# First q and k groups, first x and first masks staged in the q/k stage; V's tile set there by GpSimd

## The chip, the cores and the metric

The kernel runs on one NeuronCore of a Trainium2 chip. Its time is the device time of one execution in microseconds (us), and of several executions the median counts. Engines are named as in the profile: PE is TensorE (PEld its weight loads), DVE is VectorE, ACT is ScalarE, POOL is GpSimd, SP is SyncE, which only issues transfers here. An engine with a q behind its name (SPq, PEq) is its instruction queue.

## The reference, cut to what matters

One layer of a vision tower on an image batch `x` of 4 x 64 x 64 tokens with 64 channels, all in f32:

```
qkv = xw @ qkv_w.T + qkv_b                 # xw: windows of 8x8 tokens, 256 windows, 8 heads of 8
q, k = rope2(q), rope2(k)                  # rotated by row and column inside the window
attn = softmax(q * scale @ k.T)            # 64 x 64 scores per window and head
h = (attn @ v).reshape(...) @ proj_w.T + proj_b
h = h + selective_scan(layernorm(h), W_dbc, W_dt, b_dt, A_log, D)
h = h + one_of_32_experts(layernorm(h))    # routed by argmax
```

The change touches the seam between the first line with the rotation, and the attention.

## The kernel before, in words

The program is a row of blocks (`nc.Block`). Inside a block each engine runs its own instruction list, and they meet by semaphores. At a block's end all five engines meet at a barrier: none starts the next block before the last has finished this one.

**Block 1, the q and k stage (lines 166 to 354).** x is loaded into `h_all` and turned by PE into two SBUF arrays, `xT` (buffer `big_a`) and a column-wise copy in `u_all`. Then PE makes q and k, already rotated, in 32 steps m of two matmuls each (lines 286 and 288). Steps 0 to 15 make the first half of the tokens (q in 0 to 7, k in 8 to 15), steps 16 to 31 the second half. ACT (line 196) and DVE (line 344) each copy one half of the partitions of every step out of PSUM into `qkT` (buffer `big_bc`) and count it in `qk_act` and `qk_dve`. POOL makes the rotated weights `rot` at the block's start (lines 208 to 239) and then has nothing left. SP issues the loads and has nothing left after line 180.

**Block 2, the attention (lines 371 to 724).** It runs over 32 groups of 8 windows, in steps i from -2 to 35, with the groups overlapped: each engine's `body(i)` takes a piece of group i+1, i, i-1 and so on. For a group the order is:

- SP copies q and k of the group from `qkT` into `raw` (`fetch`, line 443: eight transfers, two slots of `raw` by the parity of the group) and x into `x_st` (`fetch_x`, line 453).
- POOL multiplies `raw` by two masks into `k_st` and `q_st` (`masks`, lines 476 and 478). The tiles have one slot, so the masks of group 1 wait for the scores of group 0.
- PE makes the scores (line 518, 16 matmuls, seen as 32 pieces in the profile), DVE takes the maximum (`top`, line 690) and subtracts it (line 695), ACT takes the exponential (line 619), PE turns the result (line 533) and ACT copies that into `prob_t` (line 627).
- PE makes V (line 582) from `x_st`, ACT copies it into `v_st` (line 638), PE multiplies by V (line 549), DVE normalises, PE turns and projects, and the group's h is stored in `h_all`.

`v_st` must hold zeros, with ones in one column per head. DVE sets that at the start of block 2 (lines 680 and 684, counted in `ones_set`), and PE and ACT wait for `ones_set` before anything else there. SP's list in block 2 starts with `fetch(0)`, `fetch(1)`, `fetch_x(0)`; from then on it is `fetch(i+1)`, `fetch_x(i)`. In PE's list the scores of group 0 come first, then V of group 0, then the first turn of group 0, then the scores of group 1.

**Blocks 3 and 4** are the selective scan and the experts. The change does not touch them.

Of the kernel before, what the change touches and what calls it, by code (L numbers as in the profile page):

```python
# [17 lines left out]
F32 = mybir.dt.float32  # L18
I32 = mybir.dt.int32
BF16 = mybir.dt.bfloat16  # L20
ALU = mybir.AluOpType
# [3 lines left out]
P = 128  # L25
# [38 lines left out]
def vit_layer(nc, x, qkv_w, qkv_b, proj_w, proj_b, w_dbc, w_dt, b_dt, a_log, d_skip,  # L64
              router_w, router_b, w1, b1, w2, b2, consts, out):
    ctx = ExitStack()
    with ctx:
# [33 lines left out]

        with ExitStack() as st1:
            def sb1(name, shape, dt=F32):
                return st1.enter_context(nc.sbuf_tensor(name, shape, dt))
# [59 lines left out]
            with nc.Block() as block:  # L166
                @block.sync
                def _(sp):
# [10 lines left out]
                    dup(sp, a_neg, a_log, scan_in)  # L179
                    sp.dma_start(wdt[:, :], w_dt).then_inc(scan_in, 16)  # L180

                @block.scalar
                def _(act):
                    for d in range(2):
                        act.dma_start(wraw[:, d, :], qkv_w[0:2 * C, :]).then_inc(w_in, 16)
                        act.dma_start(wraw2[:, d, :], qkv_w[2 * C:3 * C, :]).then_inc(w_in, 16)
                        act.dma_start(praw[:, d, :], proj_w).then_inc(w_in, 16)
                    act.dma_start(w_ext[C:C + 1, :], proj_b.rearrange("(o d) -> o d", o=1)).then_inc(row_in, 16)
                    act.dma_start(bv_col[:, :], qkv_b[2 * C:3 * C].rearrange("(d o) -> d o", o=1)).then_inc(row_in, 16)
                    act.preload_act_table_set("natural_log_exp_and_others")  # L190
# [12 lines left out]
                @block.gpsimd  # L203
                def _(pool):
# [12 lines left out]
                    for qk in range(2):  # L217
                        for eta in range(2):
                            def part(src):
                                v = src[:, qk * C:qk * C + C].rearrange("p (h e d) -> p h e d", e=2, d=4)  # L220
                                return v[:, :, eta, :].unsqueeze(1).broadcast_to([P, 8, 8, 4])

                            def trig(at):
                                v = kc[:, at:at + 32].rearrange("p (v d) -> p v d", d=4)
                                return v.unsqueeze(2).broadcast_to([P, 8, 8, 4])

                            dst = [rtmp[:, i].rearrange("p v (h d) -> p v h d", d=4) for i in range(2)]
                            pool.tensor_tensor(dst[0], part(w_qkv_t), trig(K_COSR), ALU.mult).then_inc(rot_made, 1)
                            pool.tensor_tensor(dst[1], part(w_swap), trig(K_SINR), ALU.mult).then_inc(rot_made, 1)
                            done += 2  # L230
                            pool.wait_ge(rot_made, done)
                            for w in range(2):
                                q = slice(64 * w, 64 * w + 64)
                                a, b = (rtmp[q, k].rearrange("p v (g n) -> p v g n", g=4) for k in range(2))
                                i = pool.tensor_tensor(rot[q, qk, eta, :, :, w, :], a, b, ALU.add)
                                i.then_inc(rot_made, 1)
                            done += 2
                            pool.wait_ge(rot_made, done)
                            pool.sem_inc(rot_ready, 1)

                @block.tensor
                def _(pe):
# [52 lines left out]
                def _(dve):  # L295
# [54 lines left out]
                    for b in range(2):  # L350
# [5 lines left out]

        attention(nc, dict(kc=kc, h_all=h_all, xT=xT, qkT=qkT, w_v=w_v[:, :].rearrange("p (e n) -> p e n", e=2),
                           w_out=w_out, banks=banks, psum=psum, u_all=u_all))  # L360

# [4 lines left out]
                                  spare=(w_v, w_out), w_delta=w_delta, wd=wd, b_col=b_col, d_col=d_col,  # L366
                                  a_neg=a_neg),
                         (router_w, router_b, w1, b1, w2, b2), out)


def attention(nc, t):
# [4 lines left out]
    with ExitStack() as ctx:  # L376
        def sb(name, shape, dt=F32):
            return ctx.enter_context(nc.sbuf_tensor(name, shape, dt))

        def sem(name):  # L380
            return ctx.enter_context(nc.semaphore(name))

        raw = sb("raw", [P, 2, 2, 4, WIN])
        x_st = sb("x_st", [P, 2, 2, WIN])
        q_st = sb("q_st", [P, 2, 2, P])
        k_st = sb("k_st", [P, 2, 2, 2, WIN])
# [3 lines left out]
        v_st = sb("v_st", [P, 2, 4, 2, 4, 18])  # L390
        inv = sb("inv", [P, 32])
        o_st = sb("o_st", [P, 32, 9])
        o_t = sb("o_t", [72, 4 * P])
# [5 lines left out]
        rstd = sb("rstd", [P, 4])  # L399
        xh = sb("xh", [P, 4, C])  # L400

        power_set, v_zeroed, ones_set = sem("power_set"), sem("v_zeroed"), sem("ones_set")
        qk_staged, x_staged = (sem("qk_staged0"), sem("qk_staged1")), sem("x_staged")
        k_masked, q_masked = sem("k_masked"), sem("q_masked")
# [24 lines left out]
        def first(i, lag=0):  # L429
            return i - lag <= 0  # L430

        with nc.Block() as block:
            @block.sync
            def _(sp):
                def fetch(i, par):

                    if not first(i, 1):
                        sp.wait_ge(k_masked, i - 1)
                        sp.wait_ge(q_masked, i - 1)
                    for eta in range(2):  # L440
                        for g in range(4):
                            a, b = 64 * eta + 16 * g, 32 * g + 16 * eta
                            sp.dma_start(raw[b:b + 16, par, :, :, :].rearrange("p q s k -> p q (s k)"),
                                         qkT[a:a + 16, :, bass.ds(i * 256, 256)]).then_inc(qk_staged[par], 16)

                def fetch_x(i):

                    if not first(i):
                        sp.wait_ge(v_done, i * 2)
                    a = xT[:, bass.ds(i * (2 * WIN) + i // 16 * (L // 2), L // 2 + 2 * WIN)]  # L450
                    src = bass.AP(tensor=a.tensor, offset=a.offset, ap=[list(a.ap[0]), [L // 2, 2], [1, 2 * WIN]],
                                  dep_tracking_offset=a.dep_tracking_offset)
                    sp.dma_start(x_st[:, :, :, :].rearrange("p b f k -> p b (f k)"), src).then_inc(x_staged, 16)

                def body(i, par):
                    if live(i, -1):
                        fetch(i + 1, 1 - par)
                    if live(i, 0):
                        fetch_x(i)

                steps(sp, body)

            @block.gpsimd
            def _(pool):
                pool.memset(mhalf[:, :], -0.5).then_inc(power_set, 1)
                pool.wait_ge(power_set, 1)

                def masks(i, par):

                    pool.wait_ge(qk_staged[par], i // 2 * 128 + 128)  # L470
                    if not first(i):
                        pool.wait_ge(scores_done, i * 4)
                    wide = [P, 4, 2, WIN]
                    head, win = (kc[:, at:at + 2].unsqueeze(1).unsqueeze(3).broadcast_to(wide) for at in (K_HEAD, K_WIN))
                    q, k = (raw[:, par, n].unsqueeze(2).broadcast_to(wide) for n in range(2))
                    pool.tensor_tensor(k_st[:, :, :, :, :].rearrange("p f b h k -> p (f b) h k"), k, head, ALU.mult  # L476
                                       ).then_inc(k_masked, 1)
                    pool.tensor_tensor(q_st[:, :, :, :].rearrange("p f b (w k) -> p (f b) w k", w=2), q, win, ALU.mult  # L478
                                       ).then_inc(q_masked, 1)

                def body(i, par):
                    if live(i, 3):
# [1317 lines left out]
```

## Time and profile before

| | us |
|---|---|
| median of 3 executions | 671.38 (669.72 to 671.96) |
| the profiled execution | 670.87 |
| its span in the profile | 669.1 |
| busy in the span: PE / DVE / ACT / POOL | 571.2 / 503.8 / 419.3 / 307.8 |

The profile lists for one execution when each instruction ran. Beside an instruction it says how long its engine had stood idle before it and what ended that idle time. Busy time of one stage is read from windows of the span. The stages lie roughly so: q and k stage up to 63.9 us, attention up to 337.6 us, then scan, and experts from about 452 us.

### The profile page before, as it was taken

The numbers are of one execution on the slowest core, as the hardware profiler recorded it, in microseconds if no ns is written. First come the engines' busy times: TensorE is split into PE (matmuls) and PEld (weight loads), VectorE is DVE, ScalarE is ACT, GpSimd is POOL, SyncE is SP. The second block draws the span as 40 slices with busy tenths as digits, with TensorE's granted clock in tenths as the row PEclk, the third lists the DMA queues.
The fourth block names the chain that finished last, engine by engine and source line by source line (L and its number), as shares of the span: only waits on it lengthen the run. The fifth ranks groups of instructions, "written<-read, shape, count | busy, mean of one in ns | idle before, by whom it ended". The sixth has DMA issues, their size and how long they took to land. (4 is left out here: it accounts for less than half of the span.)

```text
span 669.1 us, 18246 instructions
## 1 busy us (share of the span) xinstructions
PE 571.2 (85%) x7079; PEld 386.1 (58%) x7080; DVE 503.8 (75%) x879; ACT 419.3 (63%) x723; POOL 307.8 (46%) x352
## 2 busy tenths in 40 slices
PE   3696489999999999999775666757999999999995
PEld 3321378888888888888622122234555555555552
DVE  3798277777777777777379889977777777777772
ACT  3597277777887777787559556713555555555553
POOL 5300235555555555555369659854343332333320
PEclk9798599999999999999977688897999999999999
DMA  9500222222222222221020000000100101001011
GB/s 193 96 1 6 62 56 54 52 50 59 52 55 54 50 52 58 53 51 28 2 28 0 0 1 0 2 2 1 25 21 23 24 20 23 22 22 25 20 23 25
DMA packets 62376, 23.27 MB, mean 35 GB/s; under 512 B 45778, under 2 KB 62162, under 8 KB 62290
## 3 DMA queue, kind: packets, MB, share of 16 engines
q1 hardware_dynamic: 61472, 21.96, 16.2%
q8 instruction: 58, 0.95, 0.6%
q10 hardware_dynamic: 690, 0.13, 0.1%
q14 instruction: 28, 0.23, 0.1%
q0 software_dynamic: 128, 0.00, 0.0%
HBM read 5.29 MB, written 4.19 MB: 14 GB/s over the span
## 5 line engine op out<-in xcount | busy, mean ns | idle before, releaser
L690 DVE TENSOR_REDUCE top<-psum 128x16 f32<-128x1024 f32 x64 | 78.0, 1219 | 61.0 <-PE psum L518 61.0
L627 ACT ACTIVATE prob_t<-psum 128x512 f32<-128x512 f32 x128 | 69.6, 595 | 27.4 <-PE psum L533 27.4
L695 DVE TENSOR_TENSOR prob<-psum,top 128x1024 f32<-128x1024 f32 x64 | 78.4, 1224 | 2.2
L533 PE MATMUL psum<-kc,prob 128*128 128x128 f32 x512 | 69.9, 280 | 11.5 <-ACT prob L619 10.0
L1646 ACT ACTIVATE hid<-psum,b1c 128x512 f32<-128x512 f32 x96 | 59.0, 685 | 32.1 <-PE psum L1553 32.1
L619 ACT ACTIVATE prob<-prob 128x1024 f32<-128x1024 f32 x64 | 67.7, 1058 | 15.8 <-DVE prob L695 15.8
L484 POOL TENSOR_TENSOR rstd<-var,mhalf 128x4 f32<-128x4 f32 x32 | 32.3, 1009 | 85.8 <-DVE var L721 85.8
L1561 PE MATMUL psum<-x_t,w1x 64*64 64x256 f32 x1024 | 70.9, 393 | 0.0
L533 PEld LDWEIGHTS psum<-kc,prob 128*128 128x128 f32 x512 | 55.7, 142 | 21.1 <-ACT prob L619 19.0
L549 PEld LDWEIGHTS psum<-v_st,prob_t 128*64 128x64 f32 x2048 | 62.3, 138 | 6.2 <-ACT prob_t L627 6.1
L1536 POOL TENSOR_TENSOR m_sq<-m_xc 128x256 f32<-128x256 f32 x32 | 19.6, 614 | 99.8 <-DVE m_xc L1697 99.8
L549 PE MATMUL psum<-v_st,prob_t 128*64 128x18 f32 x2048 | 65.5, 212 | 0.0
L1634 PE MATMUL psum<-hid,w2x 128*64 128x256 f32 x512 | 61.4, 382 | 0.4 <-ACT hid L1646 0.4
L518 PE MATMUL psum<-k_st,q_st 32*128 32x128 f32 x1024 | 39.4, 292 | 12.1 <-POOL q_st L478 12.1
L1561 PEld LDWEIGHTS psum<-x_t,w1x 64*64 64x64 f32 x1024 | 33.1, 133 | 19.6 <-issue 11.7
L518 PEld LDWEIGHTS psum<-k_st,q_st 32*128 32x128 f32 x1024 | 33.1, 194 | 17.5 <-issue 17.5
L1538 POOL TENSOR_TENSOR m_rstd<-m_var,m_mhalf 128x4 f32<-128x4 f32 x32 | 32.3, 1008 | 23.6 <-DVE m_var L1711 23.6
L476 POOL TENSOR_TENSOR k_st<-raw,kc 128x512 f32<-128x512 f32 x32 | 33.3, 1042 | 20.5 <-DMA raw<-big_bc 10.3
L638 ACT ACTIVATE v_st<-psum 64x256 f32<-64x256 f32 x64 | 25.4, 398 | 27.3 <-PE psum L582 26.5
L1634 PEld LDWEIGHTS psum<-hid,w2x 128*64 128x64 f32 x512 | 33.8, 136 | 14.6 <-ACT hid L1646 0.6
L1661 ACT ACTIVATE mark_t<-psum 96x512 bf16<-96x512 f32 x32 | 19.0, 593 | 34.5 <-PE psum L1590 34.5
L1718 DVE TENSOR_SCALAR hid<-psum,b1c 128x512 f32<-128x512 f32 x32 | 24.0, 751 | 20.3 <-PE psum L1553 20.3
(200 smaller groups left out, 1280.8 us busy)
## 6 DMA issues: line engine op xcount, KB each, us to landing
raw<-big_bc SPq DMA_DIRECT2D x256, 32.0 KB, 2.0
h_all<-in_x SPq DMA_DIRECT2D x16, 256.0 KB, 5.2
x_st<-big_a SPq DMA_DIRECT2D x32, 128.0 KB, 2.2
out<-out_st SPq DMA_DIRECT2D x128, 32.0 KB
kc<-constants SPq DMA_DIRECT2D x1, 458.0 KB, 4.2
w1x<-in_L_ffn_W SPq DMA_DIRECT2D x2, 128.0 KB, 4.2
w2x<-in_L_ffn_W SPq DMA_DIRECT2D x1, 128.0 KB, 3.8
wraw<-in_L_tok_qkv_w ACTq DMA_DIRECT2D x2, 32.0 KB, 4.6
```

The lines of the kernel that those rows point to most:

```text
L476: pool.tensor_tensor(k_st[:, :, :, :, :].rearrange("p f b h k -> p (f b) h k"), k, head, ALU.mult).then_inc(k_masked, 1)
L484: pool.tensor_tensor(rstd[:, :], var[:, :], mhalf[:, :], ALU.pow).then_inc(rstd_done, 1)
L518: m = pe.matmul(banks[g][:, at:at + P], q_st[q, f, b, :], k_st[q, f, b, :, :], start=True, stop=True, skip_group_check=True)
L533: m = pe.transpose(banks[4 + half][:, n * P:n * P + P], prob[:, f, at:at + 2, :], ident)
L549: m = pe.matmul(banks[6][64 * w:64 * w + 64, at:at + 18], prob_t[:, f, n * 2 + b, 64 * w:64 * w + 64], v_st[:, par, 2 * f + b, w, n, :], s ...
L619: act.activation(prob[:, f], prob[:, f], ACT.Exp).then_inc(prob_done, 1)
L627: act.activation(prob_t[:, f, 4 * half:4 * half + 4, :].rearrange("p j q -> p (j q)"), banks[4 + half][:, :], ACT.Copy).then_inc(prob_t_do ...
L690: dve.tensor_reduce(top[:, f, :].rearrange("p (g h) -> p g h", g=4), sc, AX.X, ALU.max).then_inc(top_done, 1)
L695: dve.tensor_tensor(prob[:, f].rearrange("p (g h) k -> p g h k", g=4), sc, top[:, f, :].rearrange("p (g h) -> p g h", g=4).unsqueeze(3).br ...
L1561: m = pe.matmul(psum[64 * c:64 * c + 64, HID_BANK[g], 256 * b:256 * b + 256], w1x[q, g * 8 + 4 * c:g * 8 + 4 * c + 4, :], x_t[q, i % 2, :, ...
L1634: m = pe.matmul(psum[64 * b:64 * b + 64, 6, 0:256], w2x[:, g, :], hid[:, g, 256 * b:256 * b + 256], start=False, stop=(g == 3), skip_group ...
L1646: act.activation(hid[:, g, :], psum[:, HID_BANK[g], :], ACT.Relu, bias=b1c[:, g:g + 1]).then_inc(relu_act, 1)
```

## The change

Tiles and semaphores that both blocks now use are made outside block 1: `raw`, `x_st`, `q_st`, `k_st`, `v_st` (`sb0`, freed after the attention), and `qk_staged`, `x_staged`, `k_masked`, `q_masked`, `v_zeroed`, `ones_set`. The bodies of `fetch`, `fetch_x` and `masks` become functions `fetch_qk`, `fetch_x` and `mask_qk` without their waits. In block 1, SP waits until steps 0 to 15 of q and k are stored, and then issues both first groups' q and k and the first x. POOL sets `v_st` behind `rot`, waits for the first group's eight transfers and masks it. In block 2 these steps are left out.

```diff
@@ block 1, SP
+                    sp.wait_ge(qk_act, 16)
+                    sp.wait_ge(qk_dve, 16)
+                    for i in range(2):
+                        fetch_qk(sp, at, i)
+                    fetch_x(sp, at, 0)
@@ block 1, POOL, behind rot
+                    v_st = at["v_st"]
+                    pool.memset(v_st[:, :, :, :, :, :], 0.0).then_inc(at["v_zeroed"], 1)
+                    pool.wait_ge(at["v_zeroed"], 1)
+                    for e in range(2):
+                        ones = v_st[64 * e:64 * e + 64, :, :, :, :, 9 * e + 8:9 * e + 9]
+                        pool.memset(ones.rearrange("p a s w n o -> p (a s w n) o"), 1.0).then_inc(at["ones_set"], 1)
+                    pool.wait_ge(at["ones_set"], 2)
+                    pool.wait_ge(at["qk_staged"][0], 128)
+                    mask_qk(pool, at, 0)
@@ block 2, SP
-                def body(i, par):
-                    if live(i, -1):
-                        fetch(i + 1, 1 - par)
-                    if live(i, 0):
-                        fetch_x(i)
+                def body(i, par):
+                    if live(i, -1) and i >= 1:
+                        sp.wait_ge(k_masked, i)
+                        sp.wait_ge(q_masked, i)
+                        fetch_qk(sp, t, i + 1)
+                    if live(i, 0) and i >= 1:
                         sp.wait_ge(v_done, i * 2)
+                        fetch_x(sp, t, i)
@@ block 2, POOL
-                    if live(i, -2):
-                        masks(i + 2, par)
+                    if live(i, -2) and i >= -1:
+                        pool.wait_ge(qk_staged[par], (i + 2) // 2 * 128 + 128)
+                        pool.wait_ge(scores_done, i * 4 + 8)
+                        mask_qk(pool, t, i + 2)
@@ block 2, DVE
-                dve.memset(v_st[:, :, :, :, :, :], 0.0).then_inc(v_zeroed, 1)
-                dve.wait_ge(v_zeroed, 1)
-                for e in range(2):
-                    ones = v_st[64 * e:64 * e + 64, :, :, :, :, 9 * e + 8:9 * e + 9]
-                    dve.memset(ones.rearrange("p a s w n o -> p (a s w n) o"), 1.0).then_inc(ones_set, 1)
```

SP's list around the barrier between block 1 and block 2 (the two branches), before:

```order
L180 DMA wdt<-in_L0_attn_W_dt 16x64
L166 UNCONDITIONAL_BRANCH
L433 UNCONDITIONAL_BRANCH
L443 DMA raw<-big_bc 16x2x256 x16
L453 DMA x_st<-big_a 128x2x128
L443 DMA raw<-big_bc 16x2x256 x8
```

and now:

```order
L191 DMA wdt<-in_L0_attn_W_dt 16x64
L405 DMA raw<-big_bc 16x2x256 x16
L414 DMA x_st<-big_a 128x2x128
L177 UNCONDITIONAL_BRANCH
L486 UNCONDITIONAL_BRANCH
L405 DMA raw<-big_bc 16x2x256 x8
```

The 16 transfers of q and k and the one of x stand ahead of the branches now, and block 2 starts with the eight of group 2.

POOL's list at the same place, from the last piece of `rot` on, before:

```order
L235 TENSOR_TENSOR rot<-rtmp 64x32x8 x2
L166 UNCONDITIONAL_BRANCH
L463 UNCONDITIONAL_BRANCH
L465 MEMSET mhalf 128x4
L476 TENSOR_TENSOR k_st<-raw,kc 128x512
L478 TENSOR_TENSOR q_st<-raw,kc 128x512
```

and now:

```order
L252 TENSOR_TENSOR rot<-rtmp 64x32x8 x2
L259 MEMSET v_st 128x1152
L263 MEMSET v_st 64x64 x2
L423 TENSOR_TENSOR k_st<-raw,kc 128x512
L425 TENSOR_TENSOR q_st<-raw,kc 128x512
L177 UNCONDITIONAL_BRANCH
L499 UNCONDITIONAL_BRANCH
L501 MEMSET mhalf 128x4
L423 TENSOR_TENSOR k_st<-raw,kc 128x512
```

The three memsets of `v_st` and the masks of group 0 moved ahead of the branches; behind `mhalf` the masks of group 1 come first. The lists of PE and ACT keep their order, and DVE's loses the memsets alone.

## Rows read from the trace of the kernel before

**Rows 1.** Windows by stage: us, then each engine's busy time, PE's granted clock.

```profile
core 0: us, PE busy (x) PEld busy (x) DVE busy (x) ACT busy (x) POOL busy (x), PEclk, DMA share, GB/s
47.00:63.00 16.00, 13.42 (x58) 3.83 (x54) 15.48 (x19) 15.34 (x18) 0.00 (x0) 1.00 0.00 1
63.00:72.00 9.00, 0.00 (x0) 0.00 (x0) 1.82 (x7) 0.00 (x0) 1.41 (x3) 0.50 0.20 39
...
100.00:320.00 220.00, 213.68 (x4058) 189.79 (x4057) 171.49 (x227) 172.09 (x339) 117.02 (x140) 1.00 0.23 51
```

**Rows 2.** Timeline at the seam: start us, us, engine, line, [idle before <-releaser].

```profile
60.37 0.43 PE L291 MATMUL psum<-wdt,wd_t 16*128 16x64 f32 x2
63.47 0.17 DVE L354 TENSOR_SCALAR a_neg<-a_neg 128x16 f32<-128x16 f32 x1
63.93 10.32 SPq L443 DMA_DIRECT2D raw<-big_bc  x16
64.25 1.02 DVE L680 MEMSET v_st<- 128x1152 f32 x1 [0.60 <-PEq L166]
65.39 0.34 DVE L684 MEMSET v_st<- 64x64 f32 x2
70.69 1.04 POOL L476 TENSOR_TENSOR k_st<-raw,kc 128x512 f32<-128x512 f32 x1 [6.66 <-DMA raw<-big_bc]
71.69 1.04 POOL L478 TENSOR_TENSOR q_st<-raw,kc 128x512 f32<-128x512 f32 x1
72.87 2.09 PE L518 MATMUL psum<-k_st,q_st 32*128 32x128 f32 x32 [12.07 <-POOL q_st L478]
74.29 1.13 SPq L453 DMA_DIRECT2D x_st<-big_a  x1
75.08 1.23 DVE L690 TENSOR_REDUCE top<-psum 128x16 f32<-128x1024 f32 x1 [9.34 <-PE psum L518]
```

**Rows 3.** Timeline, first group after the seam, same columns.

```profile
75.53 5.06 SPq L443 DMA_DIRECT2D raw<-big_bc  x8
...
77.66 1.06 ACT L619 ACTIVATE prob<-prob 128x1024 f32<-128x1024 f32 x1 [14.89 <-DVE prob L695]
78.74 0.82 ACT L638 ACTIVATE v_st<-psum 64x256 f32<-64x256 f32 x2
79.70 1.94 PE L533 MATMUL psum<-kc,prob 128*128 128x128 f32 x8 [1.56 <-ACT v_st L638]
...
81.57 2.07 PE L518 MATMUL psum<-k_st,q_st 32*128 32x128 f32 x32
```

**Rows 4.** Barriers' last events: engine queue, count, durations ns, first and last start us.

```profile
L166 PEldq EVENT_SEMAPHORE  x1: 51/51/51, 63.9 to 63.9; - x1
```

```profile
L432 PEldq EVENT_SEMAPHORE  x1: 51/51/51, 337.6 to 337.6; - x1
```

**Rows 5.** Timeline behind the next barrier, attention to scan.

```profile
337.71 0.50 PEld L888 LDWEIGHTS psum<-u_all,w_delta 128*128 128x128 f32 x2 [1.10 <-issue]
```

**Rows 6.** Timeline in the q and k stage: POOL's last work, DVE's and ACT's copies.

```profile
22.57 1.53 POOL L235 TENSOR_TENSOR rot<-rtmp 64x256 f32<-64x256 f32 x2
```

```profile
32.50 14.63 DVE L344 TENSOR_SCALAR big_bc<-psum,rbias 64x512 f32<-64x512 f32 x15 [0.53 <-PE psum L288]
47.05 0.27 DVE L347 COPY wd_t<-psum 16x128 f32<-16x128 f32 x1
47.35 15.70 DVE L344 TENSOR_SCALAR big_bc<-psum,rbias 64x512 f32<-64x512 f32 x16
```

```profile
32.50 30.03 ACT L196 ACTIVATE big_bc<-psum,rbias 64x512 f32<-64x512 f32 x31 [0.94 <-PE psum L288]
```

**Rows 7.** Groups from 33 to 63 us: busy us, mean ns of one, idle before.

```profile
L344 DVE TENSOR_SCALAR big_bc<-psum,rbias 64x512 f32<-64x512 f32 x31 | 29.3, 945 | 1.6 <-PE psum L288 0.5
L196 ACT ACTIVATE big_bc<-psum,rbias 64x512 f32<-64x512 f32 x31 | 29.3, 944 | 1.7 <-PE psum L288 0.9
```

**Rows 8.** DVE's copies from PSUM, first beside POOL's `rot`, then without it.

```profile
L153 DVE COPY big_a<-psum 128x512 f32<-128x512 f32 x7 | 7.1, 1021 | 0.2
```

```profile
L153 DVE COPY big_a<-psum 128x512 f32<-128x512 f32 x2 | 2.0, 1011 | 1.1 <-PE psum L264 1.1
```

**Rows 9.** PE in narrow windows: us, PE busy, granted clock, DMA.

```profile
60.00:61.00 1.00, 0.80 (x5) 1.00 0.00 0
61.00:63.00 2.00, 0.00 (x0) 1.00 0.01 4
63.00:64.00 1.00, 0.00 (x0) 0.51 0.00 0
...
82.00:84.00 2.00, 2.00 (x36) 0.63 0.41 99
84.00:86.00 2.00, 2.00 (x55) 1.00 0.30 62
```

**Rows 10.** Timeline later in the attention, PE at its full clock.

```profile
88.18 1.06 PE L533 MATMUL psum<-kc,prob 128*128 128x128 f32 x8 [1.03 <-ACT prob L619]
89.17 1.17 PE L518 MATMUL psum<-k_st,q_st 32*128 32x128 f32 x32
```

**Rows 11.** All copies with this instruction: durations ns min/median/max, first and last start.

```profile
L690 DVE TENSOR_REDUCE top<-psum x64: 1212/1220/1225, 75.1 to 317.7; 128x16 f32<-128x1024 f32 x64
```

More of the change, by code:

```diff
@@ L99, in dup, with sb0 @@
                 eng.dma_start(dst[64 * half:64 * half + 64], src).then_inc(s, 16)
+        early = ctx.enter_context(ExitStack())
+        def sb0(name, shape, dt=F32):
+            return early.enter_context(nc.sbuf_tensor(name, shape, dt))
+        at = dict(kc=kc, xT=xT, qkT=qkT, raw=sb0("raw", [P, 2, 2, 4, WIN]), x_st=sb0("x_st", [P, 2, 2, WIN]),
+                  q_st=sb0("q_st", [P, 2, 2, P]), k_st=sb0("k_st", [P, 2, 2, 2, WIN]),
+                  v_st=sb0("v_st", [P, 2, 4, 2, 4, 18]), v_zeroed=sem("v_zeroed"), ones_set=sem("ones_set"),
+                  qk_staged=(sem("qk_staged0"), sem("qk_staged1")), x_staged=sem("x_staged"),
+                  k_masked=sem("k_masked"), q_masked=sem("q_masked"))
         with ExitStack() as st1:
@@ L354, in _ @@
                     dve.tensor_scalar(a_neg[:, :], a_neg[:, :], -1.0, None, ALU.mult).then_inc(a_done, 1)
-        attention(nc, dict(kc=kc, h_all=h_all, xT=xT, qkT=qkT, w_v=w_v[:, :].rearrange("p (e n) -> p e n", e=2),
+        attention(nc, dict(at, h_all=h_all, w_v=w_v[:, :].rearrange("p (e n) -> p e n", e=2),
                            w_out=w_out, banks=banks, psum=psum, u_all=u_all))
+        early.close()
         scan_and_experts(nc, dict(kc=kc, psum=psum, h_all=h_all, u=u_all, y=big_b, du=big_a, later=big_c,
@@ L368, in vit_layer, with fetch_qk, fetch_x, mask_qk @@
                          (router_w, router_b, w1, b1, w2, b2), out)
+def fetch_qk(sp, t, i):
+    qkT, raw, qk_staged = t["qkT"], t["raw"], t["qk_staged"]
+    for eta in range(2):
+        for g in range(4):
+            a, b = 64 * eta + 16 * g, 32 * g + 16 * eta
+            sp.dma_start(raw[b:b + 16, i % 2, :, :, :].rearrange("p q s k -> p q (s k)"),
+                         qkT[a:a + 16, :, bass.ds(i * 256, 256)]).then_inc(qk_staged[i % 2], 16)
+def fetch_x(sp, t, i):
+    a = t["xT"][:, bass.ds(i * (2 * WIN) + i // 16 * (L // 2), L // 2 + 2 * WIN)]
+    src = bass.AP(tensor=a.tensor, offset=a.offset, ap=[list(a.ap[0]), [L // 2, 2], [1, 2 * WIN]],
+                  dep_tracking_offset=a.dep_tracking_offset)
+    sp.dma_start(t["x_st"][:, :, :, :].rearrange("p b f k -> p b (f k)"), src).then_inc(t["x_staged"], 16)
+def mask_qk(pool, t, i):
+    kc, raw = t["kc"], t["raw"]
+    wide = [P, 4, 2, WIN]
+    head, win = (kc[:, at:at + 2].unsqueeze(1).unsqueeze(3).broadcast_to(wide) for at in (K_HEAD, K_WIN))
+    q, k = (raw[:, i % 2, n].unsqueeze(2).broadcast_to(wide) for n in range(2))
+    pool.tensor_tensor(t["k_st"][:, :, :, :, :].rearrange("p f b h k -> p (f b) h k"), k, head, ALU.mult
+                       ).then_inc(t["k_masked"], 1)
+    pool.tensor_tensor(t["q_st"][:, :, :, :].rearrange("p f b (w k) -> p (f b) w k", w=2), q, win, ALU.mult
+                       ).then_inc(t["q_masked"], 1)
 def attention(nc, t):
@@ L381, in sem @@
             return ctx.enter_context(nc.semaphore(name))
[L383 to L386, printed above, removed]
         top = sb("top", [P, 2, 16])
@@ L389, in attention @@
         prob_t = sb("prob_t", [P, 2, 8, P])
-        v_st = sb("v_st", [P, 2, 4, 2, 4, 18])
         inv = sb("inv", [P, 32])
@@ L400, in attention @@
         xh = sb("xh", [P, 4, C])
-        power_set, v_zeroed, ones_set = sem("power_set"), sem("v_zeroed"), sem("ones_set")
-        qk_staged, x_staged = (sem("qk_staged0"), sem("qk_staged1")), sem("x_staged")
-        k_masked, q_masked = sem("k_masked"), sem("q_masked")
+        power_set = sem("power_set")
+        q_st, k_st, x_st, v_st, ones_set, qk_staged, x_staged, k_masked, q_masked = (t[n] for n in (
+            "q_st", "k_st", "x_st", "v_st", "ones_set", "qk_staged", "x_staged", "k_masked", "q_masked"))
         scores_done, top_done, low_done, prob_done = sem("scores_done"), sem("top_done"), sem("low_done"), sem("prob_done")
@@ L434, in _ @@
             def _(sp):
[L435 to L448, printed above, removed]
-                        sp.wait_ge(v_done, i * 2)
[L450 to L453, printed above, removed]
-                def body(i, par):
-                    if live(i, -1):
-                        fetch(i + 1, 1 - par)
-                    if live(i, 0):
-                        fetch_x(i)
+                def body(i, par):
[4 more added lines that the diff above has]
+                    if live(i, 0) and i >= 1:
+                        sp.wait_ge(v_done, i * 2)
+                        fetch_x(sp, t, i)
                 steps(sp, body)
@@ L466, in _ @@
                 pool.wait_ge(power_set, 1)
[L468 to L479, printed above, removed]
                 def body(i, par):
```

## The prediction
> **What bounds the kernel now.** I read the windows by stage first [rows 1]. Between 47 and 63 us DVE and ACT are busy for over 15 of 16 us, and from 100 to 320 us PE is busy for 213.68 of 220 us. Between these two full stretches lies a hole: from 63 to 72 us PE and ACT do nothing, DVE 1.82 us and POOL 1.41 us. So I went to the timeline at this place [rows 2]. The reader is to see one chain there. The last work of the q and k stage is DVE's `a_neg`, which ends at 63.64. The barrier lets all engines go at 63.9 [rows 4]. SP issues 16 transfers of q and k from 63.93 in 10.32 us, 0.645 us each, so the first eight are issued by 69.09. POOL starts the first mask when they have landed, at 70.69, 6.76 us after SP's first issue; the second mask ends at 72.73, and PE starts the scores of group 0 at 72.87. PE had been idle for 12.07 us. From the barrier to the first matmul this is 6.8 us of transfers, 2.04 us of masks and 0.1 us of signalling, one behind the other, on the path that every later stage hangs on. DVE's memsets of `v_st` (64.25 to 65.73) lie beside it and cost nothing.
>
> **What the change does to this chain.** Its parts, one by one.
>
> 1. *The transfers start in the q and k stage.* SP waits for 16 copies of each engine. DVE's 16th ends at 47.13 (32.50 plus 14.63), just before `wd_t` [rows 6]; ACT's, the 15th of the 31 in its row, ends at 47.03 by the row's mean of 0.969 us each [rows 6]. SP has no other work there. From 47.2 it needs 10.32 us for 16 transfers and 1.13 us for x, so it is free at 58.7. That is 4.9 us ahead of DVE's last instruction at 63.64. The barrier does not move, and the issues cost nothing. If SP were slower by more than 4.9 us it would set the barrier.
>
> 2. *The masks of group 0.* With the 6.76 us from above, POOL starts them at 54.0 and ends them at 56.0, 7.6 us ahead of 63.64. No time on the path. POOL had no work there at all (0.00 us from 47 to 63 us) [rows 1].
>
> 3. *V's tile on POOL.* On DVE the memsets take until 65.73 [rows 2]. If they had stayed there, PE, which waits for `ones_set`, could not start ahead of 65.73, and this edit alone is then worth 1.6 us of the gain. On POOL no row shows a memset of this size beside DVE; the bound is from below nothing and from above the 30 us that POOL has between `rot`, which ends at 24.10 [rows 6], and the landing of q and k at 54. It costs nothing unless it slows DVE.
>
> 4. *Work beside the copies.* The new transfers, memsets and masks run beside DVE's and ACT's copies out of PSUM, and these have no slack: 29.3 of 30 us on both engines [rows 7]. So anything that slows them moves the barrier. The nearest rows say that nothing does. DVE's copy from PSUM takes 1021 ns beside POOL's work on `rot` and 1011 ns without it [rows 8]; 12 copies at that difference of 10 ns are 0.1 us. Beside the attention's transfers, with a DMA share of 0.23 [rows 1], DVE's reading of PSUM takes 1212 to 1225 ns in all 64 cases [rows 11]. I take 0 and keep 0.1. The page "SBUF — State Buffer" of the Trainium skill (section "Who interferes with whom") speaks partly against this edit: a DVE `copy` or `tensor_scalar` in a two-port mode and a GpSimd instruction exclude each other for their whole length. By that rule, if it held for line 344, two masks of 1.04 us would hold DVE for up to 2.1 us, and the gain would be 6.7 us. The same section says that a DVE instruction with at most one SBUF input outside these modes does not meet GpSimd, and that transfers never meet an engine; the 1021 against 1011 ns bears that out for copies from PSUM.
>
> 5. *The first scores.* What is left between the barrier and the first matmul is PE's own start. In the trace, PE's barrier event comes at 63.9 [rows 4]. At the next barrier it comes at 337.6 and PE's first weight load at 337.71 [rows 4, 5], so 0.1 us later. At the seam itself DVE's first instruction stands at 64.25, 0.3 us later. With three waits, all satisfied, I take 64.1, and keep 64.0 and 64.4 as ends. The gain is 72.87 - 64.1 = **8.8 us**, with ends 8.5 and 8.9.
>
> 6. *What is late next, and does the rest follow.* Distances from the start of the scores: DVE's `top` comes 2.21 us behind, ACT's exponential 4.79, the copy of V 5.87, the first turn 6.83, the scores of group 1 8.70 [rows 2, 3]. In this chain ACT's exponential (77.66 to 78.72) comes ahead of V's copy in ACT's list, and V's copy starts 0.02 us behind it, so x arriving earlier gains nothing more. Group 1's masks wait for the scores of group 0 as before, and end some 4.2 us behind their start (2.09 us of scores, 2.04 us of masks), well ahead of 8.70. The transfers of group 2 start at 63.93 and not at 75.53 [rows 3]; relative to the scores that is 0.2 us ahead instead of 2.7 us behind. Nothing in the list is later than before relative to the scores, so all that follows shifts as a piece, to the end of the kernel.
>
> **The clock.** PE's last matmul of the q and k stage ends at 60.80, and the granted clock falls at 63.0, ahead of the barrier, from 2.4 to 1.2 GHz; it comes back at 83.5, 3.8 us after PE's work became dense at 79.70 [rows 2, 3, 9]. With the change PE starts at 64.1, so it most likely starts at the low clock as well, and the shift stays whole. If the clock has not fallen, the scores of groups 0 and 1 and the first turn take 1.17, 1.17 and 1.06 us in place of 2.09, 2.07 and 1.94 [rows 2, 3, 10]: 2.7 us more gain, 11.5 in all. If it comes back after twice the 3.8 us, these 3.8 us do half their work and cost 1.9 us: gain 6.9. I take the same as before, and both ends go into the range.
>
> **The sum.** Profiled execution before: 670.87 us, of it 669.1 us span and 1.8 us around it. After: span 660.3, execution 662.1. The median of the three executions shown is 0.5 us above the profiled one, so I put the new median at 671.4 - 8.8 = **662.6 us**.
>
> **The rivals.**
>
> *The staging slows the copies (the slower side).* From 47.2 to 58.7 us the transfers read the very buffer that ACT and DVE write, and 12 copies of each engine fall into that time at 0.945 us each [rows 7]. Each nanosecond on them moves the barrier. The 8.8 us are eaten from 0.73 us per copy on; if each took twice its time, the loss were 11.3 us and the kernel would take 671.4 + 2.5 = 673.9 us. For it: no row shows these copies beside transfers, and there is no slack. Against it: the copies beside POOL and the readings of PSUM beside transfers show nothing of the kind [rows 8, 11]. Chance 0.03.
>
> *Part of the gain is lost at the start.* PE and ACT had over 9 us behind the barrier in which whatever their queues still fetch stayed hidden; now their first work is due at once. For it: DVE's first instruction comes 0.3 us behind the barrier, where SP's comes at once [rows 2]. Against it: at the next barrier PE starts after 0.1 us. If some 4 us came back this way, the time would be about 666.6 us; if the two masks of 1.04 us held DVE's copies for their whole length, 2.1 us would go, and it would be 664.7 us. Chance 0.07.
>
> *Nothing is gained.* Either the change does not do what it says, because something in the q and k stage holds the first masks until the barrier, or a later wait gives the time back. The first would need SP's wait to be met only at the stage's end: with the last copies at 63.05 (47.35 plus 15.70 [rows 6]) plus 6.76 and 2.04 us the scores would start at 72, the gain would be 0.9 us, the time 670.5 us. Against it: steps 0 to 15 are over at 47.13 [rows 6]. The second has no place in the lists that I found. Chance 0.03.
>
> *The clock does not fall, or comes back sooner.* Gain 9 to 11.5 us, 660 to 662 us. Chance 0.12.
>
> **How the numbers follow.** The forecast (gain 6.9 to 8.9 us, 662.5 to 664.5 us) has 0.75, the clock's good case 0.12, the partial loss 0.07, no gain 0.03, slower 0.03. The executions of before spread from 1.7 below to 0.6 above their median, and the new ones will too. The range takes in the forecast, the good clock and the near half of the partial loss: 660.0 to 665.5 us. Within 0.3%, which is 2.0 us and about what a measurement of this kernel can tell from no change, lie the cases without gain: 0.04 with a bit of the partial loss. Faster by more than that: 0.93. Slower by more than that: 0.03.
>
> **What would show it in the profile of after.** The window behind the barrier has scores in it: PE's first line-518 work (its new line) at 64.0 to 64.4 us, where the barrier is still at 63.9; SP's 17 issues between 47.2 and 58.7; POOL's first masks at about 54 to 56; the copies of the q and k stage still at 945 ns; the first turn still 6.8 us behind the first scores; and the barrier to the scan at 337.6 - 8.8 = 328.8 us. The prediction is wrong at step 4 if the first barrier comes later than 64.2, at step 5 if the scores start over 0.5 us behind it, at step 6 if the distances behind the scores grow, and in the clock if these distances change together with the granted clock between 64 and 85 us.

## The result

| us | before | after |
|---|---|---|
| median of 6 executions each | 671.93 (669.72 to 673.36) | 663.12 (660.82 to 663.79) |
| profiled execution | 670.87 | 661.06 |
| its span | 669.1 | 659.3 |

The ratio after to before is 0.9864, with a 95% interval from 0.9839 to 0.9888: the kernel became 9 us faster (7.5 to 10.8 by the interval). The forecast was 662.6 us and 8.8 us of gain.

### The profile after

This is the timeline at the seam in the kernel after (start us, us, engine, line, and idle time before it with what ended that). It answers [rows 2] and [rows 6].

```profile
24.39 1.06 POOL L259 MEMSET v_st<- 128x1152 f32 x1 [0.16 <-POOL rot L252]
25.50 0.47 POOL L263 MEMSET v_st<- 64x64 f32 x2
...
45.09 10.31 SPq L405 DMA_DIRECT2D raw<-big_bc  x16
55.44 0.69 SPq L414 DMA_DIRECT2D x_st<-big_a  x1
...
51.83 1.04 POOL L423 TENSOR_TENSOR k_st<-raw,kc 128x512 f32<-128x512 f32 x1 [25.85 <-DMA raw<-big_bc]
52.83 1.04 POOL L425 TENSOR_TENSOR q_st<-raw,kc 128x512 f32<-128x512 f32 x1
...
61.35 0.17 DVE L381 TENSOR_SCALAR a_neg<-a_neg 128x16 f32<-128x16 f32 x1
...
61.99 1.17 PE L543 MATMUL psum<-k_st,q_st 32*128 32x128 f32 x32 [3.32 <-PEq L177]
```

SP issues right behind DVE's and ACT's 16th copy and is free 5.4 us ahead of `a_neg`'s end. POOL's masks end at 53.87, 7.7 us ahead of it. The scores of group 0 no longer wait for a mask (`q_st`), but for the barrier (`PEq L177`), whose event stands at 61.7. From there to the first scores it is 0.3 us, where it was 9.0 us. The barrier's event in this profile, then the same event and the first scores in a second profile of the same kernel (run `e10_after_again` below):

```profile
L177 PEldq EVENT_SEMAPHORE  x1: 51/51/51, 61.7 to 61.7; - x1
```

```profile
L177 PEldq EVENT_SEMAPHORE  x1: 51/51/51, 64.0 to 64.0; - x1
```

```profile
64.29 2.09 PE L543 MATMUL psum<-k_st,q_st 32*128 32x128 f32 x32 [3.31 <-PEq L177]
```

The whole gain can be put down in four pieces, each from one barrier's event or first instruction to the next. The last column is the second profile.

| us from the span's start | before | after | after, again |
|---|---|---|---|
| first barrier | 63.9 | 61.7 | 64.0 |
| first scores | 72.87 | 61.99 | 64.29 |
| end of the attention (second barrier) | 337.6 | 327.7 | 330.0 |
| end of the scan (third barrier) | 448.5 | 438.6 | 440.9 |
| end of the span | 669.1 | 659.3 | 661.6 |
| barrier to scores | 9.0 | 0.3 | 0.3 |
| scores to end of the attention | 264.7 | 265.7 | 265.7 |
| scan, then experts | 110.9, 220.6 | 110.9, 220.7 | 110.9, 220.7 |

So the way from the barrier to the first scores became 8.7 us shorter in both profiles. The first profile shows 9.8 us of span because two other pieces moved as well: the q and k stage was 2.2 us shorter, and the attention from the first scores on 1.0 us longer. The first is TensorE's clock, as the runs below show. The second most likely is too; what speaks for that stands under "Left open". In narrow windows of the kernel after (us, PE's busy time, granted clock; compare [rows 9]) it reads:

```profile
core 0: us, PE busy (x), PEclk, DMA share, GB/s
25.00:33.00 8.00, 6.29 (x34) 1.00 0.03 2
...
61.00:63.00 2.00, 1.01 (x32) 1.00 0.00 0
63.00:64.00 1.00, 0.82 (x24) 0.81 0.28 54
64.00:73.00 9.00, 5.09 (x46) 0.50 0.29 62
...
74.00:77.00 3.00, 2.30 (x78) 1.00 0.02 5
...
78.00:80.00 2.00, 2.00 (x22) 0.50 0.32 72
...
81.00:84.00 3.00, 3.00 (x70) 1.00 0.24 50
```

The first scores still run at 2.4 GHz (1.17 us, where they took 2.09 before), then the clock falls to 1.2 GHz at 63.6, comes back at 73.9, falls again at 77.3 and is back at 80.7.

### The profile page after: what moved, and what is told of

It is laid out like the page before. It is cut to its first block and busy times, and to the rows that moved or that the text cites. A ratio compares the mean times of both kernels' runs of the same rounds, so it can differ in the third digit from the quotient of the medians.

```text
span 659.3 us, 18247 instructions
## 1 busy us (share of the span) xinstructions
PE 573.0 (87%) x7079; PEld 387.4 (59%) x7080; DVE 502.5 (76%) x876; ACT 419.9 (64%) x723; POOL 309.2 (47%) x355
## 5 line engine op out<-in xcount | busy, mean ns | idle before, releaser
L558 PE MATMUL psum<-kc,prob 128*128 128x128 f32 x512 | 71.7, 285 | 13.4 <-ACT prob L644 8.4
L558 PEld LDWEIGHTS psum<-kc,prob 128*128 128x128 f32 x512 | 57.1, 145 | 23.0 <-ACT prob L644 19.6
```

The source lines that it names most:

```text
L558: m = pe.transpose(banks[4 + half][:, n * P:n * P + P], prob[:, f, at:at + 2, :], ident)
```

## The experiments

Theory A is the prediction's: the gain is the chain of first transfers and first masks taken off the path, with V's tile moved so that it does not take the chain's place. Rival B: a good part of the gain is TensorE's clock, which happened to fall otherwise in the new order. Theory C, formed on the profile after: the clock costs some us around the seam and in the q and k stage in both kernels, and these can be had by keeping TensorE busy. Each run was timed in turn with the kernel before on one chip, and the ratios are to that.

| run | ratio (95%) | barrier | first scores behind it | scores to end of attention |
|---|---|---|---|---|
| e1_v_only | 0.9997 (0.9983 to 1.001) | 64.3 | 9.0 | 265.2 |
| e2_masks_back | 0.991 (0.9894 to 0.9926) | 63.0 | 2.5 | 264.6 |
| e3_v_on_dve | 0.9886 (0.987 to 0.9902) | 63.1 | 1.9 | 265.5 |
| e4_late_staging | 1.005 (1.0036 to 1.0064) | 74.9 | 0.3 | 265.1 |
| e5_more_beside | 0.9877 (0.9859 to 0.9896) | 63.0 | 0.2 | 264.6 |
| e6_fill | 0.9864 (0.9844 to 0.9884) | 63.0 | 0.3 | 262.8 |
| e7_fill_before | 1.0025 (1.0012 to 1.0039) | 61.6 | 12.4 | 263.0 |
| e8_fill_all | 0.9831 (0.9813 to 0.985) | 62.1 | 0.3 | 262.8 |
| e9_fill_before5 | 1.0021 (1.0004 to 1.0038) | 64.1 | 9.0 | 267.0 |
| e10_after_again | 0.9856 (0.9828 to 0.9883) | 64.0 | 0.3 | 265.7 |
| e11_fill_all_again | 0.9814 (0.9787 to 0.9842) | 62.1 | 0.3 | 262.9 |

### V's tile alone

Edit, against the kernel after: staging and first masks go back behind the barrier, the memsets stay.

```diff
@@ block 1
-                    for i in range(2):
-                        fetch_qk(sp, at, i)
-                    fetch_x(sp, at, 0)
-                    pool.wait_ge(at["qk_staged"][0], 128)
-                    mask_qk(pool, at, 0)
@@ block 2
+                for i in range(2):
+                    fetch_qk(sp, t, i)
+                fetch_x(sp, t, 0)
+                pool.wait_ge(qk_staged[0], 128)
+                mask_qk(pool, t, 0)
```

> The kernel after, with the staging and the first masks put back into the attention block; only V's tile is still set by GpSimd in the q and k stage. Theory A (the gain is the chain of first transfers and first masks taken off the path; setting V's tile was hidden beside it): no gain, ratio to before 1.000 within 0.003, scores of group 0 start 9.0 us behind the first barrier. Rival B (a good part of the gain is TensorE's clock, which happens to stay up in the new order): the clock does what chance makes it do here too, so gains of 1 to 3 us can show without any staging, together with a granted clock that does not fall at 25 us.

Measured: 671.62 us against 671.32, no gain. The scores stand 9.0 us behind the barrier and wait for the mask, as in [rows 2]:

```profile
71.11 1.04 POOL L416 TENSOR_TENSOR k_st<-raw,kc 128x512 f32<-128x512 f32 x1 [6.65 <-DMA raw<-big_bc]
...
73.30 0.59 PE L542 MATMUL psum<-k_st,q_st 32*128 32x128 f32 x4 [12.06 <-POOL q_st L418]
```

Moving work that lies beside the chain is worth nothing while the chain is there.

### The first masks put back

Edit: `mask_qk(pool, at, 0)` and its wait stand at the start of POOL's list in block 2.

> The kernel after, with the masks of group 0 alone put back behind the barrier; transfers and V's tile stay early. Theory A: the scores start 2.04 us of masks plus 0.3 us behind the barrier, 2.3 to 2.5 us in place of 0.3; the gain is 6.6 us, the ratio to before 0.990. Rival B: the distance moves the same, but the time can move by more or less than 2 us against the kernel after, as the clock falls before or after the scores' start.

Measured: 665.21 us, ratio 0.991, so 6 us of gain remain of 9. POOL's masks follow the barrier at once, and the scores follow them:

```profile
63.28 1.04 POOL L421 TENSOR_TENSOR k_st<-raw,kc 128x512 f32<-128x512 f32 x1
64.27 1.04 POOL L423 TENSOR_TENSOR q_st<-raw,kc 128x512 f32<-128x512 f32 x1
...
65.46 0.81 PE L543 MATMUL psum<-k_st,q_st 32*128 32x128 f32 x8 [5.50 <-POOL q_st L423]
```

The distance is 2.5 us (63.0 to 65.46), 2.2 us more than after: the masks' price, as the prediction had it. In this profile the experts are 1.4 us longer as well (222.0 us in place of 220.6), with a granted clock of 0.81 from 10 to 20 us behind the third barrier, where it was 0.98 before; that piece lies far behind the seam, and the masks' price is read from the distance.

### V's tile put back on DVE, behind the barrier

Edit: POOL's three memsets of `v_st` go back to the start of DVE's list in block 2.

> The kernel after, with V's tile set by VectorE behind the barrier as before; transfers and first masks stay early. Theory A: the memsets were hidden before and are not now, so the scores start 1.8 to 1.9 us behind the barrier in place of 0.3, the gain is 7.1 us, the ratio 0.989. Rival (the first matmul need not wait for V's tile in effect, since its wait is met early): 0.3 us and the full gain of 8.8 us, ratio 0.986.

Measured: 663.62 us, ratio 0.9886. The scores now wait for DVE:

```profile
63.46 1.02 DVE L698 MEMSET v_st<- 128x1152 f32 x1 [0.60 <-PEq L177]
64.59 0.34 DVE L702 MEMSET v_st<- 64x64 f32 x2
64.99 1.88 PE L536 MATMUL psum<-k_st,q_st 32*128 32x128 f32 x28 [4.98 <-DVE v_st L702]
```

1.9 us behind the barrier and not 0.3: what was hidden behind 9 us of chain is 1.6 us on the path once the chain is gone. The memsets are worth nothing alone (the run above) and 1.6 us together with the staging.

### The staging issued too late

```diff
-                    sp.wait_ge(qk_act, 16)
-                    sp.wait_ge(qk_dve, 16)
+                    sp.wait_ge(qk_act, 32)
+                    sp.wait_ge(qk_dve, 32)
```

> The kernel after, but SyncE waits for all 32 copies of each engine, not 16, before it issues the staging; everything else as after. Theory A (the cover is the second half of the copies, and only that): the first masks end 8.8 us behind the last copy, so the barrier comes 8.9 us later than in the kernel after (about 72 us by the trace of before), the scores 0.3 us behind it, and the gain is 0.5 us or nothing: ratio 0.998 to 1.001. Rival (the gain came from the shorter list behind the barrier or from other places): most of the 8.8 us stay.

Measured: 674.88 us, ratio 1.005, 3.4 us slower than before. The direction of theory A is borne out, since the whole gain is gone with the cover, but the barrier was expected at about 72 us and stands at 74.9, 3 us later. The trace shows what was left out of it:

```profile
63.28 10.30 SPq L405 DMA_DIRECT2D raw<-big_bc  x16
...
70.02 1.04 POOL L423 TENSOR_TENSOR k_st<-raw,kc 128x512 f32<-128x512 f32 x1 [43.99 <-DMA raw<-big_bc]
71.01 1.04 POOL L425 TENSOR_TENSOR q_st<-raw,kc 128x512 f32<-128x512 f32 x1
73.62 0.69 SPq L414 DMA_DIRECT2D x_st<-big_a  x1
74.96 0.11 POOL L501 MEMSET mhalf<- 128x4 f32 x1 [2.90 <-POOLq L177]
75.03 1.25 SPq L405 DMA_DIRECT2D raw<-big_bc  x2
75.15 1.24 PE L543 MATMUL psum<-k_st,q_st 32*128 32x128 f32 x16 [14.20 <-PEq L177]
```

I had counted the chain to the first masks, which ends at 72.05. But the barrier waits for SP too, and SP's list holds the second group and x as well: it ends at 74.31. In the kernel before the first scores did not wait for these, because no barrier stood between. Staging ahead of a barrier makes all of it due there, also what is needed later only.

Not all of the lost time is this. Of the 4.2 us by which this profile's span is above that of before (673.3 against 669.1), the later scores are 2.3 (75.15 against 72.87), the attention 0.3, and the experts 1.6 (222.2 us in place of 220.6). In the experts the clock came up later. From 10 to 20 us behind the third barrier, in the kernel before and then in this run:

```profile
458.50:468.50 10.00, 9.69 (x108) 0.98 0.01 2
```

```profile
461.10:471.10 10.00, 9.69 (x90) 0.78 0.00 1
```

Why the clock came up later there was not looked into.

### More work beside the copies

Edit: SP issues 4 further transfers from `big_bc` into a tile of their own and waits for them; POOL makes 4 further masks into another unused tile.

> The kernel after with more work beside the copies of the q and k stage: SyncE issues 4 further transfers from the same buffer into a tile of its own, GpSimd repeats the two masks twice more into another unused tile (4 instructions, 4 us). All of it ends ahead of the barrier by the trace of after (60.7 and 58 us against 61.4). Theory A (what runs beside the copies costs nothing): copies at 945 ns, same distance of 0.3 us from barrier to scores, ratio to before 0.986 to 0.988 as for the kernel after. Rival (transfers or GpSimd hold the copies a little): 4 further transfers and 4 further masks would show in the mean of the copies and bring the barrier later by up to 4 us.

Measured: ratio 0.9877, with an interval that holds the kernel after's 0.9864. The added masks ran, and the copies of 33 to 63 us did not get longer (busy us, mean ns, compare [rows 7]):

```profile
L377 DVE TENSOR_SCALAR big_bc<-psum,rbias 64x512 f32<-64x512 f32 x30 | 28.6, 953 | 2.0 <-PE psum L321 1.0
L216 ACT ACTIVATE big_bc<-psum,rbias 64x512 f32<-64x512 f32 x30 | 28.1, 938 | 1.8 <-PE psum L321 1.1
...
L431 POOL TENSOR_TENSOR prod<-raw,kc 128x512 f32<-128x512 f32 x4 | 4.2, 1042 | 0.2
```

953 and 938 ns against 945 and 944 before: one 8 ns longer, the other 6 ns shorter. The barrier stands at 63.0 us, as in the other profiles with the same clock in this stage (see the last runs below). With 20 raw transfers and 6 masks in that stretch, neither transfers nor GpSimd hold these copies. The slower rival of the prediction falls with it.

### TensorE kept busy at the seam

Edit, against the kernel after: matmuls of the constants against themselves into a PSUM bank that nobody reads at that time (`fill(n)` is n of 128x512, each seen as two pieces in the profile).

```diff
@@ block 1, PE, behind its last matmul
+                    fill(pe, banks[2], 3)
@@ block 2, PE, body(i)
+                    if i == 0:
+                        fill(1)          # ahead of turn(0, 1)
+                    if i == -1:
+                        fill(4)          # between values(0) and turn(0, 0)
+                    if i == 0:
+                        fill(1)          # ahead of turn(1, 0)
```

> The kernel after with useless matmuls that keep TensorE busy where it waits, their result is never read: 3 of 128x512 behind its last work in the q and k stage, 4 between the first V and the first turn, 1 ahead of the second turn, 1 ahead of the third. Theory C (the time around the seam that the change left is the clock's: the kernel after lost 1.0 us there because the clock fell at 63.6 and again at 77.3): the granted clock stays up through the seam, the scores take 1.17 us each, the distance from the first scores to the end of the attention shrinks from 265.7 to about 262 us, and the median comes 1 to 3 us under the kernel after, ratio to before 0.982 to 0.985. Rival D (the first groups are paced by VectorE and ScalarE, the clock matters little): the clock stays up and the time stays within 0.5 us of the kernel after, or the filling matmuls delay the turns.

Measured: 660.68 us against 669.85, ratio 0.9864. The clock stays up, and the scores of groups 0 and 1 take 1.17 us each:

```profile
63.26 1.17 PE L549 MATMUL psum<-k_st,q_st 32*128 32x128 f32 x32 [0.55 <-PEq L182]
64.37 0.69 PE L613 MATMUL psum<-w_v,x_st 128*64 128x64 f32 x16
64.98 3.70 PE L627 MATMUL psum<-kc 128*128 128x512 f32 x8
69.18 1.06 PE L564 MATMUL psum<-kc,prob 128*128 128x128 f32 x8 [0.50 <-ACT v_st L681]
70.17 1.17 PE L549 MATMUL psum<-k_st,q_st 32*128 32x128 f32 x32
```

From the first scores to the end of the attention it is 262.8 us, 2.9 us less than in the kernel after, 1.8 less than in the run with more work beside the copies and 1.9 less than in the kernel before. So the piece that theory C named is there in the profile. The time is less clear: the median is 0.7 us under the run with more work beside the copies, which is the nearest relative timed on that chip, the ratio sits above the expected 0.982 to 0.985, and the intervals overlap. By time alone this run does not tell C from D; by the stretch of the trace it does.

### The same filling in the kernel before

Edit: the kernel before with the same fillings, and 10 more matmuls behind the barrier while PE waits for the first masks.

> The kernel before (nothing staged early) with the same useless matmuls and 10 more of 128x512 while TensorE waits for the first masks. The hole of 9 us stays, only the clock is held up in it. Theory A and C together: the scores still start 9.0 us behind the barrier, the clock's part is the 2.7 us that the low clock cost, ratio to before 0.996. Rival B (the change gained much of its time through the clock): filling alone gives half of the 8.8 us or more, ratio 0.993 or less.

Measured: ratio 1.0025, slower. PE had not finished filling when the masks were ready:

```profile
63.52 10.54 PE L602 MATMUL psum<-kc 128*128 128x512 f32 x20 [2.21 <-DVE v_st L702]
74.00 1.17 PE L524 MATMUL psum<-k_st,q_st 32*128 32x128 f32 x32
```

The scores came 12.4 us behind the barrier in place of 9.0. The run is mis-sized as a test: it lost 3.4 us to the filling and won 1.7 us in the attention (263.0 us in place of 264.7). So I ran it again with 5.

> The kernel before with the useless matmuls of the run before it, but 5 in place of 10 behind the barrier, so that they end ahead of the first masks (the 10 took from 63.5 to 74.0 us and held the scores up by 3.4 us). Theory A and C: scores 9.0 us behind the barrier, 263 us from the first scores to the end of the attention in place of 264.7, ratio to before 0.996 to 0.998. Rival B (the clock is a good part of the change's gain): 0.993 or less.

Measured: ratio 1.0021, slower again. Now the scores stand 9.0 us behind the barrier, and the first ones run at full clock, but the clock fell behind them, and the four matmuls that were to fill the next gap ran slowly and late (5.39 us in place of the 3.70 above, the granted clock 0.50 up to 81 us):

```profile
73.08 1.17 PE L524 MATMUL psum<-k_st,q_st 32*128 32x128 f32 x32 [2.54 <-POOL q_st L484]
76.79 1.12 PE L588 MATMUL psum<-w_v,x_st 128*64 128x64 f32 x16 [2.54 <-DMA x_st<-big_a]
```

With x not yet there, V waits until 76.79, the filling starts at 77.84, and the scores of group 1 come at 84.04, 11.0 us behind the first and not 8.7. The attention took 267.0 us from the first scores. Both runs speak against rival B: nothing like the change's gain can be had in the kernel before through the clock. How much the low clock itself costs there was not measured cleanly; 1.9 us is the difference to the fully clocked run above.

### TensorE kept busy in the q and k stage as well

Edit, on top of the filling at the seam:

```diff
                     for n in range(16):
+                        if n >= 8:
+                            fill(pe, banks[2], 1, 256)
                         pe.wait_ge(x_in[rho * 4 + j], 32)
...
+                    fill(pe, banks[2], 1)
                     pe.wait_ge(x_even, 8)
```

> e6 with further useless matmuls where TensorE waits for x in the q and k stage: one of 128x256 ahead of each of the last 8 sets of turns, one of 128x512 behind them. Theory C: the clock no longer falls between 25 and 32 us, the barrier stands at 61.7 to 61.9 us in every execution (63.0 to 64.3 where the clock fell for 3.4 or 6.8 us), and the median comes another 1 to 2 us under e6, ratio to before 0.979 to 0.983, with a narrower spread. Rival: the filling delays the turns of x, and the barrier stands at 63 us or later.

> The kernel after, unchanged, beside the next one on one chip. Theory A: ratio to before 0.986 to 0.988, scores 0.3 us behind the barrier. The clock in the q and k stage and at the seam can fall or not from one execution to the next, so the barrier stands between 61.7 and 64.3 us and the executions spread over 2 to 3 us.

> The kernel with all useless matmuls once more, beside the kernel after on one chip. Theory C: 3 to 4 us under the kernel after (2.9 us at the seam, up to 2 us in the q and k stage), spread under 1.5 us, ratio to before 0.981 to 0.984. Rival (the earlier difference of 2 to 4 us was the chip's): within 1 us of the kernel after.

Measured: 658.71 us, ratio 0.9831, executions from 658.41 to 659.28; again in the later run 659.16 us, 0.9814, from 658.72 to 659.62. Beside it on that chip the kernel after had 662.39 us (660.79 to 663.55), 0.9856. So both fillings together gave 3.2 us more, and the spread of the executions went from 2.8 to 0.9 us. The granted clock from 25 to 33 us and the place of the first barrier go together in all profiles. The rows are, in this order, the kernel before, the kernel after again, the masks put back, the filled kernel, and the kernel before with the 10 matmuls behind the barrier, which has no filling in this stretch:

```profile
25.00:33.00 8.00, 6.33 (x22) 0.57 0.03 2
```

```profile
25.00:33.00 8.00, 6.17 (x22) 0.57 0.03 2
```

```profile
25.00:33.00 8.00, 6.33 (x26) 0.79 0.03 2
```

```profile
25.00:33.00 8.00, 7.19 (x36) 1.00 0.03 2
```

```profile
25.00:33.00 8.00, 6.33 (x34) 1.00 0.03 2
```

The barriers to these are at 63.9, 64.0, 63.0, 62.1 and 61.6 us; at 1.00 in the first profile of after, it was 61.7. The four profiles with 0.79 have it at 63.0 to 63.1, those with 0.60 and 0.62 at 64.1 and 64.3. The 2.2 us between the profile of before and that of after in this stage are thus the clock's, not the change's: the same kernel after shows both 61.7 and 64.0, and the order of before shows 61.6 where the clock stayed up. The filled kernel was expected at 61.7 to 61.9 and has 62.1: TensorE's first matmul for q and k starts at 28.52 us there, and at 28.14 in the first profile of after, so the fillings themselves cost 0.4 us. That is less than the clock costs where it falls.

## Why the prediction was right, point by point

**The chain.** Right. The scores waited for transfers and masks, in series, and nothing else: V's tile alone gave nothing, each part put back took its own price.

**Step 1, the transfers early.** Right. SP issued the 16 in 10.31 us beside the copies and was free 5.4 us ahead of `a_neg`'s end (4.9 said). The late staging shows the condition that the step named: SP sets the barrier when it is too late. The rival "nothing is gained" took its time for that case from the first masks alone (a gain of 0.9 us); the list's end sets the barrier 2.9 us later than that, and nothing was gained.

**Step 2, the masks.** Right. They ended 7.7 us ahead (7.6 said), and put back cost 2.2 us of distance.

**Step 3, V's tile.** Right. The memsets took 1.06 and 0.47 us on POOL at 24.4 us, under nothing; left on DVE they cost 1.6 us, as said.

**Step 4, work beside the copies.** Right with 0. In 33 to 63 us of the kernel after:

```profile
L213 ACT ACTIVATE big_bc<-psum,rbias 64x512 f32<-64x512 f32 x29 | 27.4, 945 | 0.7
L371 DVE TENSOR_SCALAR big_bc<-psum,rbias 64x512 f32<-64x512 f32 x29 | 27.4, 945 | 0.9
```

945 ns, as in [rows 7]. The page "SBUF — State Buffer" of the Trainium skill ("Who interferes with whom") lets a GpSimd instruction lock out a DVE `tensor_scalar` in a two-port mode, and not one with at most one SBUF input outside it; the copies take their data from PSUM and at most `rbias` from SBUF, and 945 ns with and without POOL's masks beside them (953 and 938 with four more) agrees with the second.

**Step 5, the first scores.** The point was 0.2 us behind the barrier, with ends 0.1 and 0.5; it is 0.3 (61.7 to 61.99, 64.0 to 64.29). The gain of the step is 8.7, not 8.8 us.

**Step 6, nothing else late.** Right. In the second profile of after the scores of group 1 come 8.70 us behind the first (64.29 to 72.99), the same distance as before, and the first turn 6.83 (71.12).

**The clock at the seam.** The expected course (low from ahead of the first scores) came in one profile and not in the other. In both, the stretch to the end of the attention was 1.0 us longer than in the profile of before. In the second profile the granted clock comes back later behind the first turn. It starts at 71.12 and the clock is back at 76.6, 5.5 us later, where it had been 3.8:

```profile
63.00:64.00 1.00, 0.00 (x0) 0.50 0.00 0
...
74.00:76.00 2.00, 2.00 (x28) 0.50 0.26 52
76.00:77.00 1.00, 1.00 (x11) 0.69 0.03 8
77.00:78.00 1.00, 1.00 (x41) 1.00 0.05 16
```

The bound of 1.9 us of loss that the prediction kept covers this. The other bound was too wide: 2.7 us for a clock that stays up, where 1.9 were measured. The sum of three shortened instructions counted them as if each stood on the path; the exponentials and DVE's steps between them do not get shorter with the clock. With the clock up, the scores of group 1 come 6.91 us behind the first (63.26 to 70.17) and not 8.70: 1.8 us, as much as the first two of the three shortened instructions; the third adds almost nothing.

**What was not foreseen.** The prediction looked at the clock at the seam alone. In the q and k stage it also falls, or not, from one execution to the next, and moves the barrier of the kernel after by 2.3 us between two profiles. This term had a row in the profile of before and was not in the range's working; only the spread of the executions stood in for it. The experts have such a term too: 222.0 and 222.2 us in two runs in place of 220.6. With terms of this size left out, the point's nearness (662.6 against 663.12) is partly luck.

**Left open.** Whether the low clock after the first scores is more frequent in the kernel after than before was not settled; both profiles of after have 265.7 us for the stretch, the kernel before 264.7, V's tile alone 265.2. That the clock, and not the new order, makes the 1.0 us is not shown, but two things speak for it. The run with more work beside the copies has the whole change in it and 264.6 us. And in the 24 us behind the first scores, added up from windows of 1 us, the clock was low for 10.2 us in that run, 10.6 in the kernel before, 11.6 with V's tile alone (265.2 us), 12.3 and 13.6 in the two profiles of after, and for none in the filled kernels (262.8 and 262.9 us). The masks put back, with 6.9 us and 264.6 us, do not fit into this row.

## What to carry to other kernels

At a barrier between two stages, look for a serial start of the second (transfer, preparation, first matmul) and for the moment at which its inputs are complete in the first: engines that are idle there can do it at no cost, as long as all that they issue ends ahead of the barrier. Move every wait in front of the first matmul together, since a step of 1.6 us that was hidden behind 9 us is worth nothing alone and stands on the path once the rest is gone. When a difference in two profiles is larger than the change explains, put the barriers' times side by side and look at the granted clock of each stretch before giving the change the credit.

## What the runs showed of the hardware that was not expected

- The clock moved the same kernel's first barrier between 61.7 and 64.0 us in two profiles, with granted clocks of 1.00 and 0.57 from 25 to 33 us. Useless matmuls in TensorE's waits there held it at 1.00 in both profiles taken; together with those at the seam they brought the spread of the executions from 2.8 to 0.9 us and the time to 659.16 us, 3.2 us under the kernel after.
- The same remedy cost time where the clock fell in spite of it: in the kernel before, fillings ahead of a waiting turn ran at 1.2 GHz for the most part (0.50 up to 81 us) and put group 1's scores 2.3 us further behind. In these runs filling paid only where it ended ahead of the wait that it filled.
